# Block-routed feed-forward of a two-layer network: the mask turned by VectorE and spread by transfers through DRAM, the router two tiles ahead

## The reference, cut to what matters

```python
def _L0_ffn_ref(x, Wr, br, W1, W2):
    N_BLOCKS = 16
    BLOCK_SIZE = 64
    TOP_K = N_BLOCKS // 4
    prob = jax.nn.softmax(xf @ Wr.T + br, axis=-1)
    _, idx = jax.lax.top_k(prob, TOP_K)
    mask = jnp.zeros((n, N_BLOCKS), dtype=xf.dtype)
    mask = mask.at[jnp.arange(n)[:, None], idx].set(1.0)
    W1b = W1.reshape(N_BLOCKS, BLOCK_SIZE, in_f)
    h = jnp.einsum('nf,ibf->nib', xf, W1b)
    h = jax.nn.gelu(h, approximate=False) * mask[:, :, None]
    W2b = W2.reshape(in_f, N_BLOCKS, BLOCK_SIZE)
    y = jnp.einsum('nib,fib->nf', h, W2b)
...
x = x + _L0_ffn_ref(_layernorm(x, axis=-1), L0_ffn_Wr, L0_ffn_br, L0_ffn_W1, L0_ffn_W2)
```

## Time and profile before

| | us |
|---|---|
| median of 3 runs | 1166.45 |
| lowest and highest run | 1161.76, 1170.42 |
| profiled execution, time | 1165.38 |
| profiled execution, span | 1163.6 |
| mean granted PE clock | 0.984 |
| PE busy | 1101.6 (95%) |
| DVE busy | 701.7 (60%) |
| ACT busy | 469.7 (40%) |
| POOL busy | 304.9 (26%) |

### The profile page before, as it was taken

The page is one execution under the profiler, slowest core; times in us unless marked ns, Lnnn a source line. Parts: engine busy times, 40 slices in busy tenths (PEclk is TensorE's granted clock), DMA queues, the critical chain, the costliest instruction groups (busy, mean ns, idle before and its releaser), DMA issues. The chain is left out here.

```text
span 1163.6 us, 32572 instructions
## 1 busy us (share of the span) xinstructions
PE 1101.6 (95%) x12600; PEld 850.6 (73%) x12601; DVE 701.7 (60%) x1802; ACT 469.7 (40%) x1361; POOL 304.9 (26%) x408
## 2 busy tenths in 40 slices
PE   7998999999999899999979999999998899999996
PEld 6776888788888678898766767777775688556664
DVE  6897646454554675555448888887876588522221
ACT  2453544353434322121155555655652566322221
POOL 1701000000000000000153646556432544434442
PEclk9899999999999999999989999999999999899998
DMA  8621000000000036000101211111104742412211
GB/s 266 184 73 35 1 1 1 0 0 0 0 0 0 1 76 199 1 0 1 38 10 32 56 50 34 55 40 42 56 22 164 236 116 43 144 32 35 36 27 11
DMA packets 60205, 61.57 MB, mean 53 GB/s; under 512 B 26862, under 2 KB 51087, under 8 KB 59628
## 3 DMA queue, kind: packets, MB, share of 16 engines
q1 hardware_dynamic: 51836, 41.35, 13.4%
q0 software_dynamic: 8304, 19.32, 6.4%
HBM read 52.33 MB, written 10.14 MB: 54 GB/s over the span
## 5 line engine op out<-in xcount | busy, mean ns | idle before, releaser
L1730 ACT ACTIVATE xattn_exps<-xattn_ps_s,xattn_top 128x256 f32<-128x256 f32 x256 | 117.8, 474 | 77.1 <-DVE xattn_top L1798 77.1
L766 PEld LDWEIGHTS attn_ps_q<-attn_xnT,w_b_q 128*128 128x128 f32 x1024 | 119.9, 194 | 12.6 <-issue 12.6
L766 PE MATMUL attn_ps_q<-attn_xnT,w_b_q 128*128 128x128 f32 x1024 | 124.5, 278 | 0.0
L1256 POOL TENSOR_TENSOR fold_last_cos<-raw_last,all_consts 64x64 f32<-64x64 f32 x1 | 0.3, 312 | 455.0 <-POOLq L1064 455.0
L820 PE MATMUL attn_ps_out<-w_b_o,attn_oT 128*128 128x256 f32 x480 | 106.5, 380 | 1.8 <-DVE all_x L1001 1.5
L820 PEld LDWEIGHTS attn_ps_out<-w_b_o,attn_oT 128*128 128x128 f32 x480 | 90.0, 190 | 15.1 <-DVE all_x L1001 2.3
L874 ACT COPY attn_qT<-attn_ps_q 128x512 f32<-128x512 f32 x64 | 38.0, 594 | 149.3 <-PE attn_ps_q L766 149.3
L1805 DVE STREAM_TRANSPOSE xattn_expsT<-xattn_exps 128x1024 f32<-128x1024 f32 x64 | 79.5, 1242 | 22.4 <-ACT xattn_exps L1730 22.4
L1795 DVE TENSOR_REDUCE xattn_raw_top<-xattn_ps_s 128x4 f32<-128x1024 f32 x64 | 77.8, 1215 | 15.7 <-PE xattn_ps_s L1622 15.7
L1622 PE MATMUL xattn_ps_s<-xattn_kT,xattn_qT 64*32 64x256 f32 x2048 | 69.9, 382 | 3.0 <-ACT xattn_exps L1730 3.0
L1632 PE MATMUL xattn_ps_o<-xattn_expsT,xattn_kv 32*64 32x256 f32 x2048 | 63.5, 380 | 4.5 <-DVE xattn_last_scores L1841 3.8
(11 more groups left out here) (361 smaller groups left out, 2311.9 us busy)
## 6 DMA issues: line engine op xcount, KB each, us to landing
xattn_inverse<-xattn_inverse_rows SPq DMA_DIRECT2D x30, 256.0 KB, 4.0
all_c<-in_ctx SPq DMA_DIRECT2D x64, 64.0 KB, 1.9
moe_gate<-in_f_gate SPq DMA_DIRECT2D x8, 512.0 KB, 8.1
moe_up<-in_f_up POOLq DMA_DIRECT2D x8, 512.0 KB, 5.1
moe_down<-in_f_down POOLq DMA_DIRECT2D x8, 512.0 KB, 5.3
xattn_v_stage<-xattn_v_rows SPq DMA_DIRECT2D x16, 136.0 KB, 2.1
xattn_v_blocks<-xattn_v_stage SPq DMA_DIRECT2D x64, 34.0 KB, 2.0
attn_v_blocks<-attn_v_stage SPq DMA_DIRECT2D x64, 34.0 KB, 1.9
```

What stands on the lines that cost most here:

```text
L766: last = nc.tensor.matmul(ps_q[g % 2][:, h * P:(h + 1) * P], wq[:, c, head * DH:(head + 1) * DH], xnT[u][:, c, :], start=(c == 0), stop=(c ...
L1730: nc.scalar.activation(exps[g % 2][:, nkeys * k:nkeys * (k + 1)], ps_s[g % 2][:, nkeys * k:nkeys * (k + 1)], ACT.Exp, bias=top[u][:, n:n + ...
```

## The change

The mask no longer passes through PE and ACT. DVE writes it into the first 16 of 32 columns of a tile that was set to zero and turns it in blocks of 32x32 (`nc.vector.transpose`), which leaves blocks x 32 tokens on each group of 32 partitions. SP stores the four groups to DRAM (16 rows of 128 tokens), waits for them, and then loads them back twice with a broadcast over 64 partitions, so that spread[u] holds the mask of each inner unit, 128x1024. Masking reads it from SBUF instead of PSUM. The router and its mask run two tiles ahead instead of one, with two xnT tiles, and down is in one piece. The weight loads move from SP's queue to POOL's, about one at each tile. The selector and its copy are gone. PE's fillers ahead of the last down write to ps_T.

```diff
+        @block.gpsimd
+        def _(pool):
+            for t, _ in zip(itertools.count(), background(pool)):
+                if t < TILES:
+                    pool.wait_ge(s["xn_ready"], t + 1)
+
+        @block.sync
+        def _(sp):
+            for t in range(TILES):
+                u = t % 2
+                sp.wait_ge(s["maskT_ready"], t + 1)
+                wait_count(sp, s[f"spread{u}"], 32 * (t // 2))
+                for b in range(TB):
+                    sp.dma_start(mask_rows[u][:, b * SEQ:(b + 1) * SEQ], maskT[b * SEQ:b * SEQ + blocks, :]).then_inc(s["mask_out"], 16)
+                sp.wait_ge(s["mask_out"], 64 * t + 64)
+                wait_count(sp, s["masked_ready"], t - 1)
+                rows = mask_rows[u].rearrange("(f h) n -> h f n", h=2)
+                for h in range(2):
+                    sp.dma_start(spread[u][64 * h:64 * h + 64, :, :], rows[h].partition_broadcast(64)).then_inc(s[f"spread{u}"], 16)
...
-            def route(t):
+            def route(t, u):
                 pe.wait_ge(s["xnT_ready"], t + 1)
+                wait_count(pe, s["mask_ready"], t)
...
             def step(i, u, live):
                 if isinstance(i, int) and i == TILES:
-                    keep_busy(2, ps_h[0])
-                if live(0):
-                    up(i)
-                if live(1):
-                    turn(i + 1)
+                    keep_busy(2, ps_T)
+                if live(0):
+                    up(i, u)
+                if live(2):
+                    turn(i + 2)
                 if live(-1):
-                    down(i - 1, 1 - u, 0)
-                if live(0):
-                    turn_mask(i)
-                if live(-1):
-                    down(i - 1, 1 - u, 1)
-                if live(0):
-                    spread(i)
-                if live(1):
-                    route(i + 1)
+                    down(i - 1, 1 - u)
+                if live(2):
+                    route(i + 2, u)
...
-                nc.vector.tensor_scalar(mask[:, :], rank[:, :], float(top_k), None, ALU.is_lt).then_inc(s["mask_ready"], 1)
+                nc.vector.tensor_scalar(mask[:, 0:blocks], rank[:, :], float(top_k), None, ALU.is_lt).then_inc(s["mask_ready"], 1)
                 router.end()
+                dve.wait_ge(s["mask_ready"], t + 1)
+                wait_count(dve, s["mask_out"], 64 * t)
+                nc.vector.transpose(maskT[:, :], mask[:, :]).then_inc(s["maskT_ready"], 1)
 
             def apply_mask(t, u):
                 dve.wait_ge(s["h_ready"], 2 * t + 2)
-                dve.wait_ge(s["spread"], t + 1)
-                nc.vector.tensor_tensor(masked[u][:, :, :].rearrange("p f t -> p (f t)"), ps_mask[:, :],
+                dve.wait_ge(s[f"spread{u}"], 16 * t + 32 - 16 * u)
+                nc.vector.tensor_tensor(masked[u][:, :, :].rearrange("p f t -> p (f t)"), spread[u][:, :, :].rearrange("p f t -> p (f t)"),
                                         hidden[u][:, :, :].rearrange("p f t -> p (f t)"), ALU.mult).then_inc(s["masked_ready"], 1)
...
             def step(i, u, live):
+                if live(0):
+                    apply_mask(i, u)
+                if live(3):
+                    normalise(i + 3)
                 if live(-1):
                     residual(i - 1)
-                if live(0):
-                    apply_mask(i, u)
                 if live(2):
-                    normalise(i + 2)
-                if live(1):
-                    choose(i + 1)
+                    choose(i + 2)
                 if isinstance(i, int) and i == -1:
                     moments.roots(dve, s["dve_roots"], EPS_LN, 1.0, LAST_TWO, x_sb)
...
-        def load_d(sp):
-            sp.dma_start(raw["qr"][:, :, :], d["d_wqr"]).then_inc(got_d, 16)
-            sp.dma_start(raw["kr"][:, :, :], d["d_wkr"]).then_inc(got_d, 16)
...
+        def load_d(pool):
+            pool.dma_start(raw["qr"][:, :, :], d["d_wqr"]).then_inc(got_d, 16)
+            yield
+            pool.dma_start(raw["kr"][:, :, :], d["d_wkr"]).then_inc(got_d, 16)
+            yield
```

103 lines of the change are left out of this document (45 added, 58 removed).

## The result

The changed kernel takes 1174.75 us in the median of 10 runs (1164.99 to 1178.44), the kernel before 1169.82 beside it (10 runs, 1161.76 to 1175.42). The ratio is 1.0054, with a 95% interval of 1.0029 to 1.0079: 3.4 to 9.2 us slower, 6.3 by the ratio and 4.9 by the medians. The forecast was 1161.8, 3.6 under the profiled execution of before (1165.4), with a range up to 1173. The change goes the other way. A ratio leaves out runs that are over 1.5% above the fastest of the same kernel.

The account below looks back on a forecast made before the run. TensorE, busy 95% of the span, was taken as the bound. Stage gain 16.8 less D0 of 12, plus 0.5 for the selector's cast, less 1.7 for the clock: 3.6 off 1165.4 gives 1161.8 us, range 1155 to 1173.

Parts of the forecast that it names:

- The steady tile: Body of the feed-forward on PE: without turn_mask and spread a tile takes 7.82 us, 0.73 less than 8.55.
- The seam of 0.07: Steady tile on PE: allowance between down and route, 0.07 us taken from 0 to 0.15.
- the third mask: Mask(2) at the stage's start: raw_o and raw_q may stretch it; nothing added, up to 4 us in the range.
- D: Time from turned mask to start of the masking product: 8.2 us taken from 7.5 to 10.3, free up to 10.4.
- The chain rival: Body tiles: D over 10.4 us, each further microsecond costs half of one per tile; 1176 at D 12.5; chance 0.09.
- The first gap: PE idle before route(1), which waits for mask(0) in one PSUM bank: about 2.7 us, counted as free.
- D0: Turned mask to masking product for the first mask, beside weight loads: 12 us, bounds 8 and 15.6.
- The price of the clock: Lower granted clock on PE after the long stall before turn(3): 1.7 us charged once.
- The sum: Whole kernel: 16.8 - 12 + 0.5 - 1.7 = 3.6 us gained, from 1165.4 to 1161.8.
- The load rival: Stage start: loads stretch the first three masks, D0 near 15.6, third mask 4 us late; 1169; chance 0.12.
- Small transfers: 128 B mask stores: the read-modify-write rule would lengthen D by an unknown amount; by the trace row 8.0 to 8.2 us.

Follow-up runs that it names:

- pieces_done_earlier: Changed kernel, all masks through DRAM, but 0.25 MB of loads at the stage's start, the rest in pieces of 450 to 770 KB behind products 0 to 12; ratio 0.9994.
- two_router_banks: Changed kernel with the router's logits of even and odd tiles in two PSUM banks; stage 148.1 us long against 147.1.
- hybrid_pieces: Changed kernel with tiles 0 and 1 masked by PE, first four loads at once, raw_o and raw_q in 512 KB pieces, selector's copy in the first stage; ratio 0.9958.
- two_tiles_by_pe: Changed kernel with the masks of tiles 0 and 1 spread by PE, the others through DRAM, all loads whole; stage 137.2 us long.
- late_loads: Changed kernel with the weight loads begun only when xn(5) is ready, then one per tile, still whole; 1171.2 us in one run.
- before_pool_loads: Kernel before the change with only the weight loads moved to POOL, one per tile, and the selector's copy one step earlier; ratio 1.0020.

## Why the prediction was wrong, step by step

**The steady tile: right.** 7.82 us were forecast, 7.69 measured. Up 3.65, turn 0.22, down 3.46, route 0.36. The seam of 0.07 isn't seen, down takes 0.05 more and route 0.11 less than forecast. From up(2) to the end of the stage this is 1.1 us less than the forecast's 113.1 (116.8 measured, with the 4.8 of the third mask).

**D in the steady tile: right in size.** 8.2 was forecast; masks turned at 471.80 and 477.89 have their products at 480.09 and 486.43, 8.3 and 8.5 us later, the second one waiting for the GELU. PE never waited for one once the large loads were through; one near the end, beside the loads of bv_row, took 13.6 us and cost PE 0.2 us at most. The chain rival (D over 10.4 tile after tile) did not come; the nearest to it is pieces_done_earlier, with D up to 13.2.

**The first gap: right.** 2.7 us forecast, 2.47 measured, free as said; two_router_banks shows it.

**D0: the step that failed first.** I took 12 us, "the middle, since the loads end inside the chain", between 8 and 15.6. It was 17.1, over the upper bound. The term that broke is the store: the bound allowed it 1.3 + 5.6 = 6.9 us up to the broadcasts and it took 11.6, while the broadcasts took 5.5 where 0.64 + 8.1 were allowed. The 5.6 was the worst landing of a store beside loads elsewhere, the 8.1 the median landing of other loads of 512 KB; neither knows what is ahead of this store. What decides is when the loads ahead land. That stood in the trace of before and is in no term of the sum: its DMA view of this stage gives raw_cq 14.5 us from issue to landing, raw_ckv 15.8. Raw_cq, issued at 425.66, then lands at 440; the broadcasts go out at 440.5 and the product 5.5 us later (5.0 in the earlier trace rows): D0 = 17. I even wrote that 3 MB take 13 us "to about 438", and still didn't make the store wait for it. This is 5.1 us of the miss.

**The price of the clock: too small.** I charged 1.7 us once, beside the sum and not inside up(2). Down(0) took 5.73 us instead of 3.62, and the small steps around it were slower: up(2) is 2.0 us later than 11.3 + D0 after the filler. The 1.7 of the sum paid for most of this; a second such loss came with the third mask.

**The third mask: the second step that failed.** "I add nothing, and up to 4 in the range." It cost 4.8 us: masking product 16.4 us behind the turned mask, because the store waited out raw_o and the broadcasts raw_q. I had let it inherit D0 = 12 with no load beside it, although the text itself has 4 MB issued at 443 and 448. With the measured 16.4 in place of 12 the same sentence gives 16.4 - 11.4 = 5.0 us; down(0) at the lower clock had already used 2.1 of them, PE idled 2.69, and the clock behind that idle time took 1.76.

**The sum.** Forecast for the stage's length: 561.3 - 424.9 = 136.4; measured 147.1, 10.8 more. D0 5.1, clock at down(0) 2.0, third mask 4.8, steady tiles -1.1: 10.8. In the whole forecast the clock's 1.7 stood beside the stage, and the stage began 1.35 us earlier instead of 0.5: the POOL instruction of the earlier trace rows takes 0.22 instead of 0.76, which is 0.54; the rest stays open. So 10.8 - 1.7 - 0.9 = 8.2 us of the miss are the sum's. Of the 12.9 us between 1161.8 and 1174.75 another 4.4 are its base: it started from the profiled execution, 1165.4, and the kernel before took 1169.82 beside the changed one.

**The rivals.** The load rival was the right one and had 0.12: its mechanism is what the runs show, its size (D0 15.6, third mask 4) was 2.3 us short; its 1169 misses the 1174.75 mostly by the base, and the range ended at 1173. Its chance should have been the forecast's, since "one load per tile now" was no argument: the gates of the first three loads open within 2 us of one another.

**Small transfers.** The Trainium skill (DMA: Bandwidth & Descriptors, Specifications) has transfers under 512 B become a read-modify-write; the rows show no price of it: four stores in 128 B pieces are followed by the broadcasts 2.7 us after the first issue, 1.3 of them issue time, where the store of the earlier trace rows took 1.72; with one store in place of four it was 2.0.

## What to carry to other kernels

In this kernel a small transfer on the critical chain cost what was ahead of it on the DMA engines, not what it carried. Before moving a chain to DRAM, list every load of the stretch with its issue and its landing in the trace of before, and let the chain's store end no earlier than the loads issued ahead of it. If the work has a start where loads must run, keep the old path through the engines for those tiles (two of sixteen here: the stage went from 142.7 to 131.8 us), and cut the rest of the loads so that one piece beside a round trip still fits its slack. Pieces of 512 KB did in the body, pieces of 640 KB and more didn't; and beside the last mask, where less is free, even 512 KB cost 2.25 us.

## What the hardware showed that I had not expected

Four stores of 2 KB, issued 3.2 us behind a load of 1.5 MB of POOL's queue, were complete 11.6 us later, 1.2 us after that load had landed; issued 1.3 us behind the same load of ScalarE's queue, they took 13.5 us and ended 0.6 us after it. The Trainium skill (DMA: Bandwidth & Descriptors, Queues, rings and completion order) says two things on this: each DMA engine takes turns between its queues, a packet of typically 9 to 17 descriptors at a time, and a transfer's completion is signalled only behind every earlier write of that engine, across its queues. The DMA view of the changed kernel, which counts small transfers of its own as packets, shows when they ran. Of the 128 in SP's queue for the first mask's stores none starts from 428 to 434 us, 119 start from 434 to 438 and 9 from 438 to 440. So the stores' own data moved only over 5 us behind their issue, which the second rule alone doesn't give. From 432 to 434 the loads have 58 of them on 16 engines that are full, about 0.6 us each. If each is one descriptor, a turn by the Trainium skill's figure is an estimated 5 to 10 us, the size of this wait; but all four stores are then through within another 4 to 5 us, less than four such turns. So the trace speaks for the turns, in part, and no run varied them.

Beside two loads of 0.1 KB each, element by element, with 6.9 us to land, a mask's stores took 8.3 us (531.79 to 540.11 in the changed kernel). It is another kind of wait: all 128 of these stores' packets start from 532.5 to 534.5, and from there to 540.1 the engines move 3 GB/s. Here the packets were not held up, the completion came late; what holds it back, no run tests.

PE's clock went to the 1.2 GHz level behind gaps of 2.47, 6.24 and 2.69 us in the changed kernel, and in hybrid_pieces behind gaps of 0.81 and 1.23 us with a down of 3.7 us between them, where the next 10 us ran at 0.60. Short gaps did not decide it by themselves. The gap of 1.23 us ahead of the fold left it at full speed in two_tiles_by_pe; in late_loads the same gap, with no other idle time for 50 us ahead of it, was followed by 1.00 for 5 us and 0.83 for the next 10; and in pieces_done_earlier gaps of 1.55 and 1.23 us were followed by the same 1.00 and 0.83. With PE's work in the order of before, the first 4 us or so of up(0) ran at 0.64 in before_pool_loads and at 1.00 in the profile of before, behind the same waits of 0.77 and 0.46 us. So the same order can get either clock; how much of the scatter of the times this is stays open.
